# Attention's score matmuls: from six bfloat16 terms on two 64-row halves of the array to three float32r terms on four 32-row strips

## The reference

```
latent = x @ Wc_down
q = (latent @ Wq_up).reshape(B, T, 16, 8);  k, v = split(latent @ Wkv_up)       # k, v: (B, T, 8), shared by all heads
att = einsum('bthd,bsd->bhts', q, k) / sqrt(8)
att = where(tril, att, -inf);  att = softmax(att, -1)
y = einsum('bhts,bsd->bthd', att, v);  return y @ Wc_proj
...
for _ in range(2):   # the experts
    z_norm = rmsnorm(z) * norm_w;  top 2 of softmax(z_norm @ router_w), normalised
    z = z + sum over e of weight_e * (silu(z_norm @ w1[e]) * (z_norm @ w3[e])) @ w2[e]
```

## Time and profile before

| | |
|---|---|
| three runs | 1351.60, 1351.73, 1356.91 us; median 1351.73 |
| span of the profiled execution, first to last instruction | 1317.6 us |
| what lies around the span, against the median | 34.1 us |
| PE, DVE, ACT, POOL busy in the span | 1206.5, 1050.7, 891.2, 482.3 us |
| PE instructions (as many weight loads again) | 11172 |

### The profile page before, as it was taken

How to read it: one execution, slowest core, us unless ns; L and a number is a source line. 1 busy time by engine, 2 the same in 40 slices (tenths; PEclk the granted TensorE clock), 3 DMA queues, 4 the chain that set the end, 5 groups by cost and what they waited for, 6 DMA issues and landing times. The chain is left out here.

```text
span 1317.6 us, 28397 instructions
## 1 busy us (share of the span) xinstructions
PE 1206.5 (92%) x11172; PEld 593.3 (45%) x11172; DVE 1050.7 (80%) x1954; ACT 891.2 (68%) x1246; POOL 482.3 (37%) x446
## 2 busy tenths in 40 slices
PE   6888998899988989798899999999899999999988
PEld 3333332333433323365555555555456544555434
DVE  4589789869898779769977799778787798787863
ACT  3668997898877888643266676666666666666666
POOL 3542554345514872320155511555025550000170
PEclk8889998999999999989999999999999999999999
DMA  6333322233332343248364544556335453233020
GB/s 224 116 117 125 106 94 101 92 109 101 100 103 94 111 132 106 93 118 233 106 183 136 174 122 117 151 139 157 87 101 160 133 142 89 72 82 105 19 64 28
DMA packets 129876, 152.88 MB, mean 116 GB/s; under 512 B 16048, under 2 KB 90800, under 8 KB 129616
## 3 DMA queue, kind: packets, MB, share of 16 engines
q1 hardware_dynamic: 111104, 127.50, 32.9%
q0 software_dynamic: 8192, 16.79, 4.3%
q10 hardware_dynamic: 10448, 6.77, 1.7%
HBM read 109.20 MB, written 41.81 MB: 115 GB/s over the span
## 5 line engine op out<-in xcount | busy, mean ns | idle before, releaser
L2887 ACT ACTIVATE ax_prob<-second_pair 128x1024 f32<-128x1024 f32 (+1 forms) x320 | 292.9, 939 | 146.4 <-PE second_pair L2840 94.4
L528 ACT ACTIVATE m_act_h<-first_pair,const 128x1024 f32<-128x1024 f32 x256 | 270.1, 1114 | 57.7 <-PE first_pair L482 44.1
L2764 DVE TENSOR_REDUCE am_top<-second_pair 128x2 f32<-128x1024 f32 (+1 forms) x192 | 222.9, 1175 | 38.6 <-PE second_pair L2718 25.5
L3019 POOL DMA_INDIRECT slot_tokens<-xn,mr_slots x128 | 124.0, 969 | 273.7 <-PE second_bank L1877 86.2
L3049 POOL DMA_INDIRECT m_back<-slot_results,mr_slots x128 | 122.2, 955 | 243.2 <-PE second_pair L2718 167.7
L482 PE MATMUL first_pair<-m_terms,w1s 96*128 96x512 bf16 x512 | 145.9, 391 | 19.6 <-ACT m_act_h L528 19.4
L2826 PE MATMUL ax_sums<-ax_prob,al_vs 128*32 128x512 f32 (+3 forms) x1536 | 161.2, 500 | 1.8 <-ACT ax_prob L2887 1.6
L494 PE MATMUL first_pair<-m_act_h,const 128*32 128x512 f32 x1024 | 130.4, 610 | 7.0 <-DVE m_prod L543 4.9
L582 POOL TENSOR_TENSOR m_both<-m_prod,m_both 128x512 f32<-128x512 f32 x64 | 86.7, 1371 | 123.8 <-DVE m_both L543 123.8
L2863 PE MATMUL second_pair<-al_qs,al_ks 51*128 51x512 bf16 (+3 forms) x768 | 115.9, 329 | 12.8 <-DVE am_top L2764 4.3
L2718 PE MATMUL second_pair<-al_ks,al_qs 48*128 48x512 bf16 (+3 forms) x768 | 116.2, 327 | 7.6 <-DVE am_top L2764 3.7
(11 more groups left out here) (396 smaller groups left out, 2515.1 us busy)
## 6 DMA issues: line engine op xcount, KB each, us to landing
m_wt<-in_experts SPq DMA_DIRECT2D x96, 384.0 KB
m_share<-shares SPq DMA_DIRECT2D x128, 256.0 KB
m_rows<-slot_tokens SPq DMA_DIRECT2D x60, 128.0 KB
slot_results<-m_y SPq DMA_DIRECT2D x60, 128.0 KB
stack<-mp_part SPq DMA_DIRECT2D x48, 128.0 KB
m_terms<-stack SPq DMA_DIRECT2D x64, 96.0 KB, 3.7
qstack<-ap_qpart SPq DMA_DIRECT2D x48, 128.0 KB
al_qs<-qstack SPq DMA_DIRECT2D x32, 192.0 KB, 3.9
```

The costliest lines, as they stand in the source:

```text
L528: A.activation(self.act_h[:, slot, :, :], banks.bank("up", n, ep)[:, :, :], ACT.Gelu, bias=self.w("b1", 4 * half + ep, 4 * half + ep + 1)) ...
L2764: V.tensor_reduce(into[:, 2 * a:2 * a + 2, at], tile[:, :, 0:n], AX, ALU.max, negate=True).then_inc(*banks.empties("max", i, m))
L2887: A.activation(dst, src, ACT.Exp, scale=SCALE).then_inc(*banks.empties("sum", i, u))
L3019: G.indirect_dma_start(self.tokens[g], bass.IndirectOffsetOnAxis(ap=self.route.slots[g][second][:, i:i + 1], axis=0), self.entry.zn(GC * g ...
```

## The change

Queries and keys are split into two parts instead of three, in the format float32r (float32 values rounded to fewer bits), with three products (hi hi, hi lo, lo hi): 3 x 8 = 24 rows, and 26 with the two parts of the maximum. With at most 32 rows a head fits on a quarter of the array's rows, so the four heads of a task now stand on partitions 0, 32, 64 and 96 (`strip(a, x)`), and there is no second plane. ScalarE writes the first part, VectorE takes the second straight from PSUM with one subtraction. The mask tables come ready-made as 16-bit data by a DMA (`masks`), laid out for 32 rows: a diagonal block now takes four mask steps of 128, 96, 64 and 32 columns for each head instead of two of 128 and 64. The packing of four heads into one use is gone: each pass of a task has 24 uses. The transposed maxima take one bank instead of a pair. The planner gets new costs and a rule (`begins`, `strips_free`) that lets two uses of different `a` run on PE at once. The wished times are not changed.

```diff
+Q_TERMS, Q_PARTS, K_PARTS = 3, (0, 0, 1), (0, 1, 0)
+STRIP = 32
...
-MROW = TERMS * AD
+MROW = Q_TERMS * AD
+QUARTERS = CH // STRIP
...
-            A.activation(self.q[c % 2], banks.bank("q", c)[:, :], ACT.Copy).then_inc(self.q_made, 1)
-            A.activation(self.q_parts[0][c % 2], banks.bank("q", c)[:, :], ACT.Copy).then_inc(*banks.empties("q", c))
+            A.activation(self.q_parts[0][c % 2].bitcast(F32R), banks.bank("q", c)[:, :], ACT.Copy).then_inc(self.q_made, 1)
...
         for c in range(NT):
-            hi, mid, lo = (q[c % 2] for q in self.q_parts)
+            hi, lo = (q[c % 2] for q in self.q_parts)
...
-            V.tensor_tensor(self.rest[0], self.q[c % 2], hi, ALU.subtract).then_inc(split, 1)
...
-            V.tensor_copy(mid, self.rest[0]).then_inc(split, 1)
...
-            V.tensor_tensor(lo, self.rest[0], mid, ALU.subtract).then_inc(split, 1)
+            V.tensor_tensor(lo.bitcast(F32R), banks.bank("q", c)[:, :], hi, ALU.subtract).then_inc(*banks.empties("q", c))
...
-            for m in range(TERMS):
-                S.dma_start(self.qstack[b, :, m * AD:(m + 1) * AD, cols], self.q_parts[ACT_PARTS[m]][half]).then_inc(self.sent[c], 16)
+            for m in range(Q_TERMS):
+                S.dma_start(self.qstack[b, :, m * AD:(m + 1) * AD, cols], self.q_parts[Q_PARTS[m]][half]).then_inc(self.sent[c], 16)
...
-PAIRS = ((0,), (1,))
-def pairs_with(n):
-    return ((0, 1),) if n <= TILE // 2 else PAIRS
-MAX_USES = [(blk, pairs, seg, n) for blk in range(QB) for seg in range(1 + blk // 4) for n in (min((blk + 1) * CH - seg * TILE, TILE),) for pairs in pairs_with(n)]
+PAIRS = (0, 1)
+MAX_USES = [(blk, a, seg, min((blk + 1) * CH - seg * TILE, TILE)) for blk in range(QB) for seg in range(1 + blk // 4) for a in PAIRS]
...
-TILES = {"sum": "rows", "max": "rows", "weigh": "columns", "maxturn": "columns", "k": "columns", "logits2": "columns",
+TILES = {"sum": "strips", "max": "strips", "weigh": "columns", "maxturn": "columns", "k": "columns", "logits2": "columns",
...
+        def begins(key, engine):
+            if engine != "PE":
+                return engine_free.get(engine, 0.0)
+            if self.strips[key] is None or switches(key, engine):
+                return max(strips_free)
+            return max(issued, strips_free[self.strips[key]])
...
-    score = {128: 0.06, 256: 0.115, 384: 0.17, 512: 0.225}
-    longest = {128: 0.62, 256: 1.15, 384: 0.88, 512: 1.14}
+    score = {128: 0.11, 256: 0.115, 384: 0.17, 512: 0.225}
+    masked = 0.17
+    longest = {128: 0.34, 256: 0.6, 384: 0.88, 512: 1.14}
...
-            for half in range(2):
-                src = self.qstack[b, g * HG:(g + 1) * HG].rearrange("(a h) r t -> h r a t", h=2)[half]
-                S.dma_start(self.qs[64 * half:64 * half + MROW, i % Q_SLOTS, :, :], src).then_inc(self.q_landed[i % Q_SLOTS], 16)
+            for h in range(HG):
+                S.dma_start(self.qs[STRIP * h:STRIP * h + MROW, i % Q_SLOTS, :], self.qstack[b, g * HG + h]).then_inc(self.q_landed[i % Q_SLOTS], 16)
...
-    def keys_queries(self, i, blk, a, half, seg, n):
-        rows = slice(64 * half, 64 * half + MROW)
-        return self.loads.qs[rows, i % Q_SLOTS, a, blk * CH:(blk + 1) * CH], self.loads.ks[rows, (i // NG) % 2, seg * TILE:seg * TILE + n]
-    def tensor(self, ready):
+    def keys_queries(self, i, blk, a, x, seg, n):
+        rows = self.loads.strip(a, x)
+        return (self.loads.qs[rows, i % Q_SLOTS, blk * CH:(blk + 1) * CH].bitcast(F32R),
+                self.loads.ks[rows, (i // NG) % 2, seg * TILE:seg * TILE + n].bitcast(F32R))
...
-                for a in pairs:
-                    first = a * (TILE // 2) if len(pairs) > 1 else 0
-                    for x in range(2):
-                        p = E.matmul(banks.bank("max", i, m)[:, x, first:first + n], *self.keys_queries(i, blk, a, x, seg, n), start=a == pairs[0], stop=True, skip_group_check=True)
+                for x in range(2):
+                    p = E.matmul(banks.bank("max", i, m)[:, x, 0:n], *self.keys_queries(i, blk, a, x, seg, n), start=True, stop=True, skip_group_check=True)
                 if seg == blk // 4:
-                    e.wait_ge(ready, 11)
-                    for queries in range(2):
+                    e.wait_ge(masks_here, 16)
+                    for n32 in range(QUARTERS):
                         for x in range(2):
-                            p = self.forbid(banks.bank("max", i, m), x, queries, len(pairs) > 1, n - CH)
+                            p = self.forbid(banks.bank("max", i, m), a, x, n32, n - CH)
...
-    def forbid(self, tile, x, queries, both, off):
-        half = CH // 2
-        rows, first = slice(half * x, half * x + half), half * queries
-        place = self.k.bf["ident" if queries == x else "swap"][rows, :]
-        later = self.k.bf["later_t" if queries == x else "later_s"][rows, first:CH]
-        if both:
-            dst, later = tile[:, x, :].rearrange("p (a n) -> p a n", a=2)[:, :, off + first:off + CH], later.unsqueeze(1).broadcast_to([half, 2, CH - first])
-        else:
-            dst = tile[:, x, off + first:off + CH]
-        return self.k.nc.tensor.matmul(dst, place, later, start=False, stop=True, skip_group_check=True)
+    def forbid(self, tile, a, x, n32, off):
+        rows, first = self.loads.strip(a, x, STRIP), STRIP * n32
+        return self.k.nc.tensor.matmul(tile[:, x, off + first:off + CH], self.k.masks[rows, 0, n32, :], self.k.masks[rows, 1, n32, first:CH],
+                                       start=False, stop=True, skip_group_check=True)
...
-                for a in pairs:
-                    first = a * (TILE // 2) if len(pairs) > 1 else off
-                    for x in range(2):
-                        rows = slice(64 * x, 64 * x + MROW + 3)
-                        p = E.matmul(tile[:, x, first:first + n], self.loads.ks[rows, b % 2, blk * CH:(blk + 1) * CH],
-                                     self.loads.qs[rows, i % Q_SLOTS, a, th * TILE + off:(th + 1) * TILE], start=a == pairs[0], stop=True, skip_group_check=True)
+                for x in range(2):
+                    rows = self.loads.strip(a, x, MROW + 2)
+                    p = E.matmul(tile[:, x, off:TILE], self.loads.ks[rows, b % 2, blk * CH:(blk + 1) * CH].bitcast(F32R),
+                                 self.loads.qs[rows, i % Q_SLOTS, th * TILE + off:(th + 1) * TILE].bitcast(F32R), start=True, stop=True, skip_group_check=True)
                 if blk >= 4 * th:
-                    for keys in range(2):
+                    for n32 in range(QUARTERS):
                         for x in range(2):
-                            p = self.forbid(tile, x, keys, len(pairs) > 1, off)
+                            p = self.forbid(tile, a, x, n32, off)
...
-            hi, mid, lo = (q[0:nr, :] for q in self.parts[i % 2])
...
-            V.tensor_copy(hi, self.rows[0:nr, :]).then_inc(self.split, 1)
...
-            V.tensor_tensor(self.rest[0:nr, :], self.rows[0:nr, :], hi, ALU.subtract).then_inc(self.split, 1)
...
-            V.tensor_copy(mid, self.rest[0:nr, :]).then_inc(self.split, 1)
...
-            V.tensor_tensor(lo, self.rest[0:nr, :], mid, ALU.subtract).then_inc(self.split, 1)
+            hi, lo = (q[0:nr, :] for q in self.parts[i % 2])
...
+            V.tensor_tensor(lo.bitcast(F32R), banks.bank("turn", i)[0:nr, 0:CH], hi, ALU.subtract).then_inc(*banks.empties("turn", i))
...
+    masks = np.stack([(col_ == key).astype(f32), np.where(col_ > key, f32(-1e30), f32(0)), np.where(col_ < key, f32(-1e30), f32(0))], axis=1)
```

More of the change, by code:

```diff
@@ L2126, in run @@
                 if since is not None:
[L2127 removed]
+                    start, other = max(since, begins(key, engine)), switches(key, engine)
                     if engine == "PE":
@@ L2141, in run @@
             at[key] = start
+            if engine == "PE":
+                issued = start
+                strips_free = [start + takes if self.strips[key] in (None, n) else strips_free[n] for n in range(2)]
             engine_free[engine] = start + takes
```

231 lines of the change are left out of this document (99 added, 132 removed).

## The result

| | before | after | ratio [95% interval] |
|---|---|---|---|
| first comparison, one chip | 1352.31 us (4 runs) | 1445.22 us (4 runs) | 1.0692 [1.0657, 1.0726] |
| repeated on another chip (e9, e10) | 1323.05 us (7 runs) | 1405.93 us (4 runs) | 1.0653 [1.0579, 1.0726] |

The change makes the kernel 83 to 93 us slower. The forecast was slower by 25 us (1377), with a range to 1420: the direction held, the size and the range did not.

A forecast was written before the change was run, and what follows sets the result against it. PE was taken as the bound, from about 600 us on the sum of its array's steps. Terms +7 + 28 + 29 + 11 + 4 - 74 + 25 - 5 = +25 us on 1351.7 gave 1377 us, range 1335 to 1420.

The forecast's parts named there:

- the clock: PE's matmuls: every column was costed at 2.4 GHz, full clock, with no term for a lower clock.
- The switches between ways of cutting the array: PE's order: 767 switches instead of 718, at 0.09 us each, +4 us.
- the uses: PSUM banks: 24 + 24 uses per task instead of 20 + 20 undo a third of the overlap, +25 us.
- Overlap: Two pairs of heads on different strips run together: at best -74 us, less 25 for full banks, about -50.
- The rival without overlap: PE's matmuls wait until all before have started, or banks are never free: 49 us more, 1426 us; chance 0.12.
- Score columns: Score matmuls on PE: same columns, one pass if float32r streams like bfloat16, so no change from 122.9 us.
- Masks: Diagonal blocks on PE: 512 mask sets at 0.14 instead of 0.085 us, +28 us.
- Float32r: Score matmuls: weight loads +29 us entering stretches, +11 behind masks; narrow scores +7 us.
- VectorE -20 us, covered: VectorE's splits, casts and reductions: some 20 us less busy, hidden beside PE.
- The start: Sends and split of queries and keys: first scores about 10 us sooner, of which -5 us was taken.
- PE's waits: PE's waits for am_top and ax_prob: to grow from about 21 us to 40 or so.

The follow-up runs named there:

- e9: The kernel before, unchanged, run on the same chip as the repeat of the change: 1323.05 us.
- e10: The changed kernel, unchanged, run on one chip with the kernel before: 1405.93 us, ratio 1.0653.
- e15: The kernel before on its halves, packing taken away (one pair of heads per use, 24 uses per pass), planned anew: ratio 1.0208.
- e16: The kernel before on its halves, with four mask steps instead of two and the packing taken away: ratio 1.0335.
- e11: The changed kernel with bfloat16 operands (upper 16 bits) and both pairs of heads on one pair of strips: 1399.42 us, ratio 1.0572.
- e1: The changed kernel with score matmuls reading only the upper 16 bits of their operands as bfloat16: 1356.85 us, ratio 1.0250.
- e13: The kernel before without masks, its score matmuls reading 24 and 27 rows on quarters of the array: ratio 0.9994.
- e4: The kernel before without any mask matmul: ratio 0.9881.
- e5: The changed kernel with both pairs of heads read from one pair of strips, so they cannot overlap: 1519.16 us, ratio 1.122.
- e2: The kernel before with its operands read as float32r, on the old halves with old masks and order: ratio 1.0277.
- e6: The kernel before with score matmuls reading 33 rows of each half instead of 48 and 51: ratio 0.9994.

## Why the prediction was wrong

The runs form a path from before to after, each step one difference (us = ratio on 1323 us; a step is uncertain by 5 to 10 us; the half clock is that of the two profiles, in us after 580):

| step | kernels | measured | half clock | forecast |
|---|---|---|---|---|
| packing gone, 24 uses | before to e15 | +28 | 20 to 29 | 0 |
| four mask steps | e15 to e16 | +17 | 29 to 25 | +28 |
| on strips: quarters, fewer splits, new costs | e16 to e11 | +31 | 25 to 90 | -1 |
| the two pairs beside each other | e11 to e1 | -43 | 90 to 55 | -49 |
| float32r | e1 to e10 | +53 | 55 to 91 | +47 |
| sum | | +86 | 20 to 91 | +25 |

Two steps of the prediction failed; each had been put at nothing. The two rows in which they stand make 60 of the 61 us by which the sum is off; the errors of the other rows nearly cancel.

- **The first step that failed: the clock.** The sum took every column at 2.4 GHz, which is full clock as the trace of before shows it: from 780 to 880 us, at a granted clock of 1.00, the records of the masks last 216 ns (L2736) and 215 (L2840) with 128 columns, 270 and 267 with 256, so 128 columns more take some 53 ns, 2.4 columns a ns. It did so because PE stood at full clock in the earlier trace rows and would stay as busy. It did stay busy, but with 24 and 26 rows on strips instead of 48 and 51 on halves, and the time at half clock rose by 71 us on one chip (e9, e10). At e13's 0.33 us each this is an estimated 23 us (14 to 36 by the bounds of that price). It enters with the strips: e16 to e11 has 65 us more at half clock, an estimated 21 of its 31 us. The remaining 10 us may belong to e11 and not to the change. From one score matmul of 512 columns to the next it is 239 ns in e11, but 226 in e16, in e4 and also in e13, which is on quarters like e11. What e11 alone does is to read every second 16-bit value. 13 ns for 768 uses are an estimated 10 us; they would go from this row to the one of float32r. No run tests it. The switches between ways of cutting the array (forecast 4) weren't measured by themselves.
- **The second step that failed: the uses.** For 48 instead of 40 uses per task the prediction took a loss of 25 us, but only as a third of the overlap of the two pairs that full banks would undo. That the uses cost time without any overlap has no term. In e15, on the old halves, where the two pairs don't run beside each other (from one use of 512 columns to the next it is 226 ns in the median; on different strips, in the change, it is 7), they cost 27.5 us. That the two numbers agree is luck: they stand for different things.
- **Overlap: right.** In the change PE starts matmuls on other strips while earlier ones still run: where no mask stands between, two uses of 512 columns start 7 ns apart in the median. The rival without overlap, by which a matmul waits until all before it have started, is refuted by the row at 891.59, ahead of six masks that stand before it. The forecast was 74 - 25 = 49 us, e11 to e1 gives 43, of which an estimated 12 are the clock's (35 us less at half clock). In float32r it is 70 us (e5), of which the clock has an estimated half.
- **Score columns: right.** One pass. With float32r 128 columns more lengthen a record by 58 ns (medians 322 ns at 128 columns, 497 at 512), with bfloat16 by 56 (227 and 395 in e1).
- **Masks: right in kind, too dear.** The time of a set up to the next score matmul grew from 88 to 156 ns (medians of e15 and e16), 35 us for 512 sets, but 17 us come out at the end. Where the rest goes wasn't settled; PE idles 7 us less in e16 than in e15, so that part of it stands where PE had waited.
- **Float32r: the sum right, its parts not.** The prediction charged 315 entries and 127 places behind masks, and took the loads of all other uses as hidden. In the change nine in ten matmuls carry the 0.10 us, part of it beside the other pair's stream, and an estimated 12 of the 53 us are the clock's (36 us more at half clock). So the term depends on where it is measured: 37 us on halves (e2), 53 with the overlap, 85 without. The load itself takes 181 ns in the change and, in bfloat16, 92 in e1.
- **VectorE -20 us, covered: right. The start:** the first score matmul starts 11 us earlier than in the first trace of before (593.6 against 604.8 us), as forecast, and 25 us earlier on one chip (581.4 against 606.7). What of it reaches the end was not measured by itself.
- **PE's waits: wrong.** They were to grow to 40 us and are 32; in the change the whole of the longer span is PE's busy time.

## What to carry to other kernels

Price an array's step with all that it holds: its stream, its weight load wherever nothing hides it, and its clock. Moving the same columns to a smaller piece of the array, with fewer rows, cost 1.1% here through the clock (e4 to e13; an estimated 23 us, 1.7%, in the change), although the engine was as busy as before (within 3 us in each of the three windows). Packing several results into one pair of banks is worth its own term (2% here, e15), even where the waits in the profile before are small (12.4 us in e9). And give each term the run that measures it: a sum of two errors can look like one term that came true.

## What the runs showed of the hardware

- **A busy PE lost its clock.** In the change PE was busy for 30.51 of 31 us (731 to 762) at a granted clock of 0.68. The same score columns on quarters with 24 and 27 rows instead of halves with 48 and 51 (e4 to e13) took the time at half clock from 26 to 72 us. On halves with 33 rows (e6) the mean granted clock was 0.963 against 0.965 for the kernel before on that chip, and no loss in time was measured.
- **Float32r** streamed in one pass like bfloat16: one record for each matmul, of 322 to 497 ns in the change against 227 to 395 in e1 for 128 to 512 columns. Its weight load took about as long as float32's (181 ns in the change; float32 192 in the earlier trace rows, bfloat16 92 in e1).
- **The weight load of a bfloat16 mask wasn't hidden behind a float32r score matmul.** In the change the mask's load starts only with the mask's matmul, 0.28 us after the score matmul (891.57 and 891.29); in the kernel before it starts 0.01 us after it. The loads in the change, then before (at the earlier trace rows):

```profile
891.57 0.10 PEld L2804 LDWEIGHTS second_pair<-masks 32*128 32x128 bf16 x2
891.58 0.18 PEld L2825 LDWEIGHTS second_pair<-al_qs,al_ks 26*128 26x128 f32 x1
```

```profile
900.50 0.10 PEld L2736 LDWEIGHTS second_pair<-bf_later_t,bf_ident 64*128 64x128 bf16 x1
```

  The second pair's float32r load, too, starts only at 891.58, with the first mask, although no other matmul started on its strips after the first pair's scores at 891.29. e2 and e1 take the type away by itself. e2 is the kernel before with float32r scores, in the same order on the same halves, and the mask's load comes late in it; e1 is the change with bfloat16 scores, and it comes early (384 columns in both):

```profile
918.88 0.44 PE L2718 MATMUL second_pair<-al_ks,al_qs 48*128 48x384 f32 x2
919.16 0.09 PEld L2736 LDWEIGHTS second_pair<-bf_later_t,bf_ident 64*128 64x128 bf16 x1
```

```profile
872.38 0.34 PE L2825 MATMUL second_pair<-al_qs,al_ks 26*128 26x384 bf16 x2
872.39 0.32 PEld L2804 LDWEIGHTS second_pair<-masks 32*128 32x128 bf16 x8
```

  The medians say the same: 0.01 us from a score matmul of 384 columns to the mask's load in the kernel before and in e1, 0.26 us in e2 and 0.28 in the change. In e2 no mask's load behind a score matmul starts early (the shortest time is 0.11 us, behind 128 columns). So the delay comes with the type in these runs; what it costs by itself wasn't measured.
- **Chips differ**: the same kernel takes 1323 us on two of the chips and 1352 us on another, while the change's ratio is 1.065 and 1.069. The granted clock differs too, 0.973 against 0.965 on the mean of before's runs.
